# Gated cross-attention block: the last six weight-sum rounds four head slots apart in place of three, and the second product of every set in the queries' accumulator bank

## The reference

```python
q = (hidden_q @ Wq).reshape(b, lq, h, dh)
k = (hidden_kv @ Wk).reshape(b, lk, h, dh)
v = (hidden_kv @ Wv).reshape(b, lk, h, dh)
score = jnp.einsum('bqhd,bkhd->bhqk', q, k) * scale + position_bias
...
ctx = jnp.einsum('bhqk,bkhd->bqhd', probs, v).reshape(b, lq, h * dh)
return ctx @ Wo
...
x = x + jnp.tanh(g_xattn[0]) * _L0_xattn_ref(_layernorm(x, axis=-1), ctx_4096, ...)
x = x + jnp.tanh(g_ffn[0]) * _L0_ffn_ref(_layernorm(x, axis=-1), ...)
```

## Time and profile before

| | |
|---|---|
| median of 3 runs | 1742.51 us (1741.34 to 1743.66) |
| the profiled execution | 1742.19 us, span 1740.4 us |
| TensorE busy | 1709.2 us, 98% |
| VectorE, ScalarE, GpSimd busy | 71%, 40%, 52% |
| DMA, share of 16 engines (queue of SyncE) | 66.5% |
| granted TensorE clock, mean | 0.995 |

### The profile page before, as it was taken

The page is one execution under the profiler, slowest core; times in us unless marked ns, Lnnn a source line. Parts: engine busy times, 40 slices in busy tenths (PEclk is TensorE's granted clock), DMA queues, the critical chain, the costliest instruction groups (busy, mean ns, idle before and its releaser), DMA issues.

```text
span 1740.4 us, 25729 instructions
## 1 busy us (share of the span) xinstructions
PE 1709.2 (98%) x8522; PEld 1441.5 (83%) x8522; DVE 1227.3 (71%) x2648; ACT 693.0 (40%) x1473; POOL 899.8 (52%) x1187
## 2 busy tenths in 40 slices
PE   8999999999999999999999999999999999999998
PEld 7888888888888888888888878888888888888886
DVE  5677767777676665666667767578777777777675
ACT  5555555554344442444333433233333333333331
POOL 5767777764476564555355553254533434333331
PEclk9999999999999999999999999999999999999999
DMA  7777777766667765658667866486766666666541
GB/s 276 273 260 260 275 268 279 275 240 218 224 226 263 233 219 183 233 201 295 237 236 271 292 237 231 148 295 246 260 236 235 216 224 242 227 213 243 198 145 43
DMA packets 162856, 407.95 MB, mean 234 GB/s; under 512 B 15554, under 2 KB 56642, under 8 KB 162724
## 3 DMA queue, kind: packets, MB, share of 16 engines
q1 hardware_dynamic: 162580, 406.05, 66.5%
q10 hardware_dynamic: 144, 0.26, 0.1%
HBM read 313.97 MB, written 92.27 MB: 233 GB/s over the span
## 4 chain that ended last, share of the span: by engine, by line
PE 79%; DVE 8%; issue 4%; POOL 4%; ACT 2%; DMA 2%; SPq 0%; DVEq 0%; ACTq 0%; POOLq 0%
PE vo_bank L394 11%; PE vo_bank L396 11%; PE vo_bank L395 11%; PE q_bank L394 6%; PE q_bank L396 6%; PE q_bank L395 6%; PE k_bank L394 5%; PE k_bank L396 5%; PE k_bank L395 5%; PE pv_two L399 4%; PE s_two L399 4%; DVE score L1231 2%; DVE pv_two L1211 2%; PE pv_two L400 1%; PE s_two L400 1%
## 5 line engine op out<-in xcount | busy, mean ns | idle before, releaser
L1513 POOL TENSOR_TENSOR score<-score,row_max 128x256 f32<-128x256 f32 x128 | 78.6, 614 | 560.1 <-DVE row_max L1236 560.1
L1424 POOL TENSOR_TENSOR ot_lo<-attn,ot_hi 128x512 fp32r<-128x512 f32 x128 | 165.7, 1294 | 178.3 <-ACT ot_hi L926 178.3
L1022 ACT ACTIVATE attn<-pv_two 128x512 f32<-128x512 f32 x128 | 76.5, 597 | 386.6 <-PE pv_two L400 386.5
L394 PE MATMUL q_bank<-xt_hi,wq 128*128 128x512 f32 x512 | 209.4, 409 | 0.0
L396 PE MATMUL q_bank<-xt_hi,wq 128*128 128x512 f32 x512 | 201.2, 393 | 0.0
L395 PE MATMUL q_bank<-xt_lo,wq 128*128 128x512 f32 x512 | 200.8, 392 | 0.0
L394 PE MATMUL k_bank<-ct_hi,wk 128*128 128x512 f32 x512 | 199.5, 390 | 0.1
L395 PE MATMUL k_bank<-ct_lo,wk 128*128 128x512 f32 x512 | 199.3, 389 | 0.0
L396 PE MATMUL k_bank<-ct_hi,wk 128*128 128x512 f32 x512 | 199.3, 389 | 0.0
L394 PE MATMUL vo_bank<-wo,ot_hi 128*128 128x512 f32 x496 | 193.2, 389 | 0.9 <-POOL ot_lo L1424 0.9
L396 PE MATMUL vo_bank<-wo,ot_lo 128*128 128x512 f32 x496 | 193.1, 389 | 0.0
(11 more groups left out here) (211 smaller groups left out, 4073.3 us busy)
## 6 DMA issues: line engine op xcount, KB each, us to landing
wq<-wq_split SPq DMA_DIRECT2D x96, 512.0 KB, 3.3
wk<-wk_split SPq DMA_DIRECT2D x96, 512.0 KB, 3.6
wo<-wo_split SPq DMA_DIRECT2D x96, 512.0 KB, 5.5
wv<-wv_mixed SPq DMA_DIRECT2D x32, 1024.0 KB, 7.4
wv<-wv_split SPq DMA_DIRECT2D x24, 1024.0 KB, 6.5
raw_bias<-in_pair_bias SPq DMA_DIRECT2D x64, 256.0 KB, 5.8
wq_split<-wq SPq DMA_DIRECT2D x32, 512.0 KB, 2.9
wk_split<-wk SPq DMA_DIRECT2D x32, 512.0 KB, 4.1
```

The lines of the kernel that those rows point to most:

```text
L394: pe.matmul(to, left[0], right[0], start=first, stop=False)
L1022: act.activation(by(attn, PB), pv_two[:, :, 1, :], ACT.Copy).then_inc(ot_b, 1)
L1424: pool.tensor_tensor(to, src, f32(of), ALU.subtract).then_inc(done, 1)
L1513: pool.tensor_tensor(score[:, :, :], score[:, :, :], row_max[:, :].unsqueeze(2).to_broadcast([P, PB, S]), ALU.subtract).then_inc(shift_don ...
```

## The change

Two edits. The last six weight rounds stand in slots 60, 64, 68, 72, 76 and 80 in place of 60, 63, 66, 69, 72 and 75; the ten before them (33 to 49 in steps of two, and 55) and the four context rounds (52, 57, 84, 89) stay. And more product tiles go to the queries' bank: until now (6,1) and, except in the last set, (3,1); now also (1,1) and (4,0), so that in each slot with products the second product is in `q_bank`. In the first set, whose products 1 and 2 stand two in a slot, it is their first tile, (1,0) and (2,0), that goes there.

```diff
-T_ROUNDS = [*range(33, 50, 2), 55, *range(60, 76, 3)]
+T_ROUNDS = [*range(33, 50, 2), 55, *range(60, 81, 4)]
...
 def in_query_bank(u, p, t):
 
-    return (p, t) == (6, 1) or (p, t) == (3, 1) and u < PAIRS - 1
+    if u == FIRST_PAIR and p in (1, 2):
+        return t == 0
+    return (p, t) in ((1, 1), (6, 1), (4, 0)) or (p, t) == (3, 1) and u < PAIRS - 1
```

## The result

| | before | changed |
|---|---|---|
| median | 1742.53 us (4 runs, 1741.34 to 1743.66) | 1725.01 us (4 runs, 1724.61 to 1725.29) |
| profiled span | 1740.4 us | 1723.4 us |
| mean granted clock, profiled | 0.995 | 0.999 |

The ratio is 0.9899, with an interval from 0.9882 to 0.9917: faster by 1.0%, 17.5 us; 1724.3 were forecast.

A forecast was written before the change was run, and what follows sets the result against it. TensorE, busy 98% of the span, was taken as the bound, so its waits count. Gains of 4.4 + 6.5 + 4.6 + 1.1 + 1.2 + 0.4 = 18.2 us take 1742.5 to 1724.3 us; range 1721.5 to 1731.

The forecast's parts named there:

- What bounds the kernel: TensorE, busy 98% of the span: only its waits matter, four lines totalling 11.3 us, plus a lower clock behind the long ones.
- The rounds: Rounds four slots apart remove the waits for late loads: 4.4 us in slots 64 and 65, 6.5 us in slot 76.
- The cover of `v_lo`: In slots with outputs, `v_lo` ends at about 10.6 us, the attention starts at 11.9: 1.3 us of cover, nothing paid.
- The banks: Product tiles no longer share banks: 4.6 us in slots 72 to 120, 1.1 in 84 and 108, 1.2 in 61 and 62.
- The 0.4 us of traces: Slots 68, 92, 100 and 116 keep a trace of the same bank wait, 0.1 us each.
- Where the stall goes: The mix is late only against the next slot; `v_lo` keeps 1.3 us of cover, so nothing is paid.
- The sum of 18.2: All gains together, 4.4 + 6.5 + 4.6 + 1.1 + 1.2 + 0.4 us, giving 1724.3 us.
- Loads of product weights: Rival: loads for product 2 come late in a few of 15 slots, giving back 3 to 8 us; chance 0.09.
- The bank half gives nothing: Rival: VectorE's order holds the slots together, `ot_lo` late by more than 1.1 us; 7.3 us stay, about 1731.6; chance 0.05.
- `q_lo`: Rival: 17 tiles now wait for `q_lo`; beyond 1.5 us late, each us costs 17; 1750 at 3 us; chance 0.02.
- The clock: Rival: TensorE loses its clock in each of 15 changed product slots, 25 us on top, 1750; chance 0.02.

The follow-up runs named there:

- run 1: Kernel before with only the late rounds moved to four slots apart, its banks as before: 1732.19 us, ratio 0.9949.
- run 5: Changed kernel with its late rounds one slot earlier, in 59, 63, 67, 71, 75 and 79: 1729.02 us.
- run 2: Banks as changed, but the late rounds three slots apart as in the kernel before: 1733.70 us, ratio 0.9949.
- run 12: Changed kernel with each late round's piece loaded in the next slot, behind that slot's query weights: 1734.39 us, ratio 0.9958.
- run 6: Changed kernel with SyncE loading each late round's piece in the round's own slot, not the slot before: 1725.32 us.
- run 3: Changed kernel with product tile (4,0) back in the vo pair: 1730.80 us.
- run 4: Changed kernel with product tile (1,1) back in the vo pair: 1726.74 us.
- run 7: Changed kernel with the first of the two products ahead of the scores, not the second, in the queries' bank: 1724.08 us.
- run 9: The changed kernel once more, unaltered, on the chip of run 10: 1724.37 us.
- run 8: Changed kernel with VectorE's statistics in slots 25, 57 and 89 put between its two emptyings of outputs: 1723.19 us.
- run 10: Changed kernel with the next block's statistics in slots 21 and 22 of a block in place of 22 and 25: 1721.84 us.
- run 11: Changed kernel with statistics in slots 21 and 22 of a block and the first product, not the second, in the queries' bank: 1722.61 us.

## Why the prediction was right

- **What bounds the kernel** held: four waits, the clock behind two of them, and a restart of some 0.2 us behind each short one. The idle time of the earlier trace rows is 11.3 us and the gain was 17: whoever had added up the waits would have missed a third of it. Counting each slot against one with the same matmuls caught it.
- **The rounds** held in size: 10.95 us in slots 64, 65 and 76 against 10.9, and run 1 has 10 us from them alone. The mechanism held in its parts but not in their weight. I had called it "more important" that no mix stands in slots 63 or 75. Run 5 has its mixes there again, with the piece in time, and slots 64 and 76 lose 0.8 us; run 2, with the same banks and late pieces, loses 4.8 us more. So the waits for the load were the larger part, and the forecast came out because both went at once. The cover of `v_lo` (1.3 us) is confirmed twice, by the trace and by run 12, which used it up. What I had left open was why the load is late; the rows of SyncE beside run 6 show it, two times the save of the second half and once the product weights.
- **The banks** held: 4.6, 1.1 and 1.35 us against 4.6, 1.1 and 1.2, and runs 3 and 4 give (4,0) and (1,1) their parts; the two tiles in slots 61 and 62 were only taken back with all the others, in run 1, where both slots last 16.64 again.
- **The 0.4 us of traces was wrong.** The 0.08 us between the busy time and the length of slot 92 was no bank wait: it is there still. A rest that small had no row of its own, and should have been no term.
- **"Where the stall goes" was incomplete.** I looked at what is late next for the mix, and not for the slots that the banks shorten: slot 89 gave back 0.67 us. The sum of 18.2, less these 0.67, less the 0.4 of traces and less 0.3 in the first slots, is 16.8; the rest to the measured 17.0 is that slots 61, 62, 64 and 65 gained 0.2 more than forecast.
- **The rivals.** *Loads of product weights*: fell; slots 72 and 76 have a DMA share of 1.04 and no wait for a load. The Trainium skill, "DMA: Bandwidth & Descriptors", section "Issuing engines are not separate DMA queues", has all transfers share the same 16 engines; in this trace the sharing made TensorE wait for no load. *The bank half gives nothing*: fell, run 1 against the whole. *`q_lo`*: fell, run 7 with room to spare. *The clock*: fell, 0.998 to 0.999 in all four executions; and the profiled clock was 1.00 in every slot from 4 on. The Trainium skill, "TensorE: Matmul & The Clock Gate", section "A second HAM failure mode: psum-queue depth-cycling", reports a kernel whose cycling through banks made the clock swing; the third bank in the cycle did nothing of the kind here.

## What to carry to other kernels

Price a stall by the length of its stretch against a twin stretch with the same work, not by its idle time: where the clock falls behind it, that can cost as much again (1.64 us beside a wait of 1.59 in run 12). Give a periodic job enough distance that its input is there in time, and the save that frees its buffer has landed before the next load; here that was the larger part. Then place it where its consumer is late in the slot and its other buffers are free; the distance alone (run 5) doesn't see to that. After every saved microsecond, ask which engine's chain was anchored in the stretch that became shorter, since the next stretch then meets that chain earlier, as in slot 89.

## What I had not expected of the hardware

**A wait's length didn't decide whether the clock fell.** It fell after waits of 1.95 and 4.22 us (before, slots 64 and 76), and of 1.43 and 1.71 us (run 12, slots 65 and 69), and stayed at 1.00 after 2.44 and 2.66 us (run 2's profiled execution), after 2.22 us (run 5, slot 61), and after 1.34 and 1.45 us (run 12, slots 73 and 77). In run 2 the same program ran with a mean clock from 0.995 to 0.999, 6 us apart. A fall cost 1.64 us where two windows isolate it. What else decides was not settled. The kernel before ran from 1738.2 to 1744.2 us over all chips, at 0.995 to 0.998. Long waits alone don't explain such scatter: run 1, whose profiled execution has no wait over 1.5 us after the first slots, ran from 1730.9 to 1736.9, the longest at 0.996, and run 3, without one either, from 1727.8 to 1732.3 at 0.999 to 0.997. Where the clock fell in those executions was not recorded.

**The first slots vary by themselves, and a longer wait there need not cost time.** Windows of slots 2 and 3, first of the kernel before, then of the changed one:

```profile
37.64:49.80 12.16, 10.03 (x43) 8.46 (x42) 7.43 (x19) 7.33 (x15) 11.01 (x13) 0.78 0.89 304
49.80:62.80 13.00, 13.00 (x66) 11.06 (x66) 8.61 (x18) 7.38 (x15) 8.38 (x10) 0.98 0.91 325
```

```profile
37.34:49.43 12.09, 8.36 (x43) 7.03 (x42) 7.88 (x20) 7.25 (x15) 10.51 (x12) 0.94 0.87 316
49.43:63.09 13.66, 13.66 (x67) 11.51 (x66) 8.41 (x18) 7.38 (x15) 8.88 (x11) 0.93 0.89 317
```

The instructions are the same. In the changed kernel's execution the clock fell later, TensorE came earlier to the scores of slot 2, and waited 3.7 us for them, not 2.1: that is the whole growth of the first line of the waits. The scores began at 46.8 and 46.6 us. From the start of slot 0 to that of slot 4 it took 44.30 us, before 44.14. Run 9 is the changed kernel unaltered and had the short wait, 2.1 us, and 44.17 us: so it is not the edit. Over all executions the short wait (before; runs 1, 6, 8, 9, 10 and 12, and 2.3 us in run 2) and the long one (after; runs 3, 4, 5, 7 and 11) go across the edits; these four slots took 44.1 to 44.3 us, but 42.8 in run 2 and 45.1 in runs 4 and 11, so that two profiled spans can differ by 1 to 2 us through them alone. What sets the moment at which the clock falls there was not settled.
